# Token setup of an early-fusion kernel: GpSimd rounds the angles and makes V, the third magnitude is made with the other two, and its sine group goes first

## The reference

```python
dt = jnp.exp(log_dt)                          # 256 channels
w = -jnp.exp(log_w_real) + 1j * w_imag        # 256 x 64
dtA = w * dt[:, None]
Cm = Cc * (jnp.exp(dtA) - 1.0) / w            # Cc: 8 x 256 x 64, complex input
K = jnp.einsum('chn,hnl->chl', Cm, jnp.exp(dtA[:, :, None] * jnp.arange(512)))
h = 2 * K.real                                # 8 x 256 x 512
...
h = concatenate([h, txt], axis=1)             # 8 x 384 x 512
h = h + attention(layernorm(h)); h = h + experts(layernorm(h))
```

## Time and profile before

| | |
|---|---|
| Median of 3 runs | 885.98 us (883.85 to 888.88) |
| Profiled execution | 892.42 us, of which the span in the trace is 890.6 |
| Busy in the span | PE 775.7, DVE 509.7, ACT 366.0, POOL 344.2 us |
| PE's first matmul of the chunks | 73.75 us after the start of the span |

### The profile page before, as it was taken

How to read it: one execution, slowest core, us unless ns; L and a number is a source line. 1 busy time by engine, 2 the same in 40 slices (tenths; PEclk the granted TensorE clock), 3 DMA queues, 4 the chain that set the end, 5 groups by cost and what they waited for, 6 DMA issues and landing times.

```text
span 890.6 us, 19870 instructions
## 1 busy us (share of the span) xinstructions
PE 775.7 (87%) x7181; PEld 489.7 (55%) x7182; DVE 509.7 (57%) x927; ACT 366.0 (41%) x637; POOL 344.2 (39%) x356
## 2 busy tenths in 40 slices
PE   0007999879989999999999789999999999999993
PEld 0007998655455455564554446666666666666661
DVE  7997755786884756667744425453444444444441
ACT  4772423425225261443323324554444444444440
POOL 0036765051280030300267614444444545454441
PEclk9999999999999999999999999999999999999997
DMA  5011216134164051967524254454544444554442
GB/s 204 0 47 49 71 44 228 48 88 117 59 145 93 30 156 40 211 168 181 117 70 129 75 170 77 81 91 79 93 73 92 73 92 75 90 77 88 81 72 35
DMA packets 67645, 84.76 MB, mean 95 GB/s; under 512 B 37664, under 2 KB 37792, under 8 KB 66944
## 3 DMA queue, kind: packets, MB, share of 16 engines
q0 software_dynamic: 14080, 29.53, 19.0%
q1 hardware_dynamic: 41408, 31.42, 13.0%
q10 hardware_dynamic: 12096, 22.94, 9.6%
HBM read 48.43 MB, written 27.63 MB: 85 GB/s over the span
## 4 chain that ended last, share of the span: by engine, by line
PE 75%; DVE 12%; ACT 5%; issue 2%; POOL 2%; another core or an unknown queue 2%; DMA 2%; DVEq 0%; ACTq 0%; POOLq 0%
PE PS L2137 11%; PE PS L2139 11%; PE PS L2138 11%; PE PS L1101 8%; PE PS L1103 8%; PE PS L1102 7%; PE PS L607 7%; PE PS L2147 3%; PE PS L762 2%; PE PS L2169 2%; DVE big L1020 1%; DVE big L1457 1%; DVE work L1462 1%; PE PS L1314 1%
## 5 line engine op out<-in xcount | busy, mean ns | idle before, releaser
L2137 PE MATMUL PS<-big,work 128*128 x605 | 200.4, 331 | 3.7 <-ACT work L2215 2.4
L2139 PE MATMUL PS<-big,work 128*128 x605 | 200.8, 332 | 0.0
L2138 PE MATMUL PS<-big,work 128*128 x605 | 200.6, 332 | 0.0
L2256 DVE SCALAR_TENSOR_TENSOR work<-work,PS 128x352 f32<-128x352 f32 x55 | 28.7, 521 | 150.8 <-PE PS L2139 150.8
L2324 POOL DMA_INDIRECT out_dram<-work x55 | 88.2, 1604 | 59.4 <-DVE work L2294 49.0
L2215 ACT ACTIVATE work<-PS 128x1024 f16<-128x1024 f16 x55 | 56.3, 1023 | 86.0 <-PE PS L2147 86.0
L1706 POOL DMA_INDIRECT slots_dram<-work x48 | 50.1, 1043 | 84.8 <-DVE work L2053 62.5
L2137 PEld LDWEIGHTS PS<-big,work 128*128 128x128 f16 x605 | 59.2, 98 | 42.3 <-issue 7.2
L2139 PEld LDWEIGHTS PS<-big,work 128*128 128x128 f16 x605 | 59.2, 98 | 41.9 <-issue 0.6
L2138 PEld LDWEIGHTS PS<-big,work 128*128 128x128 f16 x605 | 59.1, 98 | 36.0 <-issue 0.6
L2311 POOL DMA_INDIRECT big<-x_dram,work x55 | 54.7, 995 | 46.6 <-POOL work L2308 44.8
(11 more groups left out here) (276 smaller groups left out, 1652.0 us busy)
## 6 DMA issues: line engine op xcount, KB each, us to landing
work<-in_weights ACTq DMA_DIRECT2D x31, 272.0 KB
work<-in_shared ACTq DMA_DIRECT2D x28, 256.0 KB, 3.3
big<-in_weights ACTq DMA_DIRECT2D x25, 272.0 KB, 3.3
x_dram<-big SPq DMA_DIRECT2D x24, 256.0 KB, 2.4
out_dram<-big SPq DMA_DIRECT2D x24, 256.0 KB, 4.6
big<-in_weights SPq DMA_DIRECT2D x1, 2176.0 KB, 10.3
big<-in_par SPq DMA_DIRECT2D x1, 1185.0 KB, 10.3
big<-in_c_real SPq DMA_DIRECT2D x1, 1024.0 KB, 5.5
```

The source lines that it names most:

```text
L2137: pe.matmul(out, x_high, w_high, start=start, stop=False)
L2138: pe.matmul(out, x_high, w_low, start=False, stop=False)
L2139: return pe.matmul(out, x_low, w_high, start=False, stop=stop)
L2256: v.scalar_tensor_tensor(a, a, 1 / (X_SCALE * W_SCALE * W_SCALE), PS[:, UB[u], 0:F], ALU.mult, ALU.mult).then_inc(m.mul, 1)
```

## The change

`kt`, the rounding, goes from DVE to POOL for all three groups; DVE keeps `gt`. `V`, three instructions of 2,048 columns (now `A2`, `B2`, `V`), goes from DVE to POOL as well; DVE keeps the three of `U`. The partial products go to tiles of their own (`V_SUB`, `U_ADD`, which are the two buffers of `P1`). `MAG_B` is made straight after `MAG_ZW`, ahead of the table of sines. The groups are taken in the order 2, 0, 1. The waits follow: POOL's `cos2` waits for ACT's cosine of group 2; DVE's multiplications wait for each group's cosine; DVE's first `P1` waits for POOL's `cos2`, its first `P2` for `sin2`, its second `P1` for `V`.

```diff
@@ -222,6 +222,7 @@
         assert R2 + 10 * Q <= NB * BLK
         SA = [cut(work, k * H, H) for k in range(16)]
         P1 = [cut(work, 16 * H + u * Q, Q) for u in range(2)]
+        V_SUB, U_ADD = P1
         assert Q == HC * PW
 
 
@@ -249,17 +250,16 @@
         def htile(i, w):
             return htok[:, slot_of(i, w), :]
 
-        GROUPS = range(3)
+        GROUPS = (2, 0, 1)
         set_v = steps("set_v", [
             "xk", "xk2", "xf", "xf2", "xnum", "xden", "xrec", "xe", "xbits", "x", "rho", "rho8", "rho64", "s", "k", "k2", "s1", "s2", "s3", "r", "r2"]
             + [f"{x}{k}" for k in "zw" for x in ("n", "m", "f")]
             + ["a2", "b2", "m2", "im2", "den", "rden", "em", "sh2", "emsh", "t2", "er", "t3", "ei", "p1", "p2", "p3", "Dr", "p4", "p5", "p6", "Di",
                "al0", "al1", "be0", "be1"]
-            + [f"{x}{g}" for g in GROUPS for x in ("kt", "gt")]
-            + ["A1", "A2", "B1", "U", "B2", "V"] + [f"{x}{g}" for g in range(2) for x in ("sin", "cos")])
-        set_a = steps("set_a", ["xt", "th", "mag_zw", "sh", "ch"] + [f"t{g}" for g in GROUPS]
-                      + [f"{x}{g}" for g in GROUPS for x in ("sin", "abs", "cos")] + ["mag_b"])
-        set_g = steps("set_g", ["wsum", "cos2", "sin2"])
+            + [f"gt{g}" for g in GROUPS] + ["A1", "B1", "U"] + [f"{x}{g}" for g in range(2) for x in ("sin", "cos")])
+        set_a = steps("set_a", ["xt", "th", "mag_zw", "mag_b", "sh", "ch"] + [f"t{g}" for g in GROUPS]
+                      + [f"{x}{g}" for g in GROUPS for x in ("sin", "abs", "cos")])
+        set_g = steps("set_g", ["wsum"] + [f"kt{g}" for g in GROUPS] + ["A2", "B2", "V", "cos2", "sin2"])
         wb_a = steps("wb_a", ["kv_sum", "kv_mean", "kv", "c_sum", "c_mean", "c", "wb"])
         wb_p = steps("wb_p", ["wb"])
         CHUNKS = range(NCHUNK)
@@ -290,7 +290,8 @@
             sp.dma_start(par, a["par"]).then_inc(s_par, 16)
             sp.dma_start(rope, a["rope"]).then_inc(s_rope, 16)
             sp.dma_start(gate_T[:], a["gate_T"]).then_inc(s_gate, 16)
-            sp.wait_ge(set_v.sem, set_v.at("V"))
+            sp.wait_ge(set_g.sem, set_g.at("V"))
+            sp.wait_ge(set_v.sem, set_v.at("U"))
             sp.dma_start(htok[:, 22:24, :], a["txt"][:, 0:2, :]).then_inc(s_txt[0], 16)
             sp.dma_start(TXT_T0.rearrange("p a t -> p (a t)"), a["txt_T"][:, 0:AW * P]).then_inc(s_txt_T[0], 16)
 
@@ -300,6 +301,9 @@
             sp.wait_ge(cm_p.sem, cm_p.at("c0"))
             sp.dma_start(TXT_T1[:, 1:3].rearrange("p k a t -> p (k a t)"), a["txt_T"][:, 2 * AW * P:]).then_inc(s_txt_T[2], 16)
             sp.dma_start(htok[:, 12:22:3, :], a["txt"][:, 4:8, :]).then_inc(s_txt[2], 16)
+
+        def over_b(x):
+            return x.unsqueeze(2).broadcast_to([P, H, B])
 
         def by_8(x):
             return x.rearrange("p (h a) -> p h a", a=AW)
@@ -313,13 +317,16 @@
             for j in range(AW):
                 last = act.activation(by_8(MAG_ZW)[:, :, j], RHOB[:, 0:2 * H], ACT.Exp, scale=float(j))
             last.then_inc(set_a.now("mag_zw"), 1)
+            for j in range(AW):
+                last = act.activation(by_8(MAG_B)[:, :, j], RHO, ACT.Exp, scale=float(j))
+            last.then_inc(set_a.now("mag_b"), 1)
 
             act.wait_ge(set_v.sem, set_v.at("r2"))
             act.wait_ge(s_early, 16)
             act.activation(SH, R, ACT.Sin, scale=SIN_PI).then_inc(set_a.now("sh"), 1)
             act.activation(CH, R, ACT.Sin, scale=SIN_PI, bias=ec("half_pi_low")).then_inc(set_a.now("ch"), 1)
-            act.wait_ge(set_v.sem, set_v.at("fw"))
             for g in GROUPS:
+                act.wait_ge(set_v.sem, set_v.at(("fz", "fw", "r2")[g]))
                 for j in range(AW):
                     out = by_8(TURN[:, g * Q:(g + 1) * Q])[:, :, j]
                     if g == 2:
@@ -334,10 +341,6 @@
                 act.activation(TURN[:, part], KT[:, part], ACT.Abs).then_inc(set_a.now(f"abs{g}"), 1)
                 act.wait_ge(set_a.sem, set_a.at(f"abs{g}"))
                 act.activation(COS[:, part], TURN[:, part], ACT.Sin, scale=-2 * SIN_PI, bias=ec("half_pi")).then_inc(set_a.now(f"cos{g}"), 1)
-            for j in range(AW):
-                last = act.activation(by_8(MAG_B)[:, :, j], RHO, ACT.Exp, scale=float(j))
-            last.then_inc(set_a.now("mag_b"), 1)
-
             act.wait_ge(s_par, 16)
             act.wait_ge(set_g.sem, set_g.at("wsum"))
             for x, part, mean in (("kv", pc("to_kv"), ec("centre_kv")), ("c", pc("compress_T"), ec("centre_c"))):
@@ -416,8 +419,18 @@
         def tok_gpsimd(pool):
             pool.wait_ge(s_par, 16)
             pool.tensor_tensor(pc("out_res_T"), pc("to_kv"), pc("out_res_T"), ALU.add).then_inc(set_g.now("wsum"), 1)
-            pool.wait_ge(set_v.sem, set_v.at("V"))
+            for g in GROUPS:
+                part = slice(g * Q, (g + 1) * Q)
+                pool.wait_ge(set_a.sem, set_a.at(f"t{g}"))
+                pool.tensor_scalar(KT[:, part], TURN[:, part], MAGIC, MAGIC, ALU.add, ALU.subtract).then_inc(set_g.now(f"kt{g}"), 1)
+            pool.wait_ge(set_v.sem, set_v.at("be1"))
+            pool.wait_ge(s_c, 32)
+            pool.tensor_tensor(hc(V), hc(CR), over_b(BE), ALU.mult).then_inc(set_g.now("A2"), 1)
             pool.wait_ge(set_a.sem, set_a.at("mag_b"))
+            pool.tensor_tensor(hc(V_SUB), hc(CI), over_b(AL), ALU.mult).then_inc(set_g.now("B2"), 1)
+            pool.wait_ge(set_g.sem, set_g.at("B2"))
+            pool.tensor_tensor(V, V, V_SUB, ALU.subtract).then_inc(set_g.now("V"), 1)
+            pool.wait_ge(set_a.sem, set_a.at("cos2"))
             pool.tensor_tensor(B1, B1, MAG_B, ALU.mult).then_inc(set_g.now("cos2"), 1)
             pool.tensor_tensor(B2, B2, MAG_B, ALU.mult).then_inc(set_g.now("sin2"), 1)
             pool.wait_ge(set_v.sem, set_v.at("cos1"))
@@ -543,39 +556,36 @@
             v.tensor_scalar(BE[HALF:P], X1[HALF:P], -1.0, None, ALU.mult).then_inc(set_v.now("be1"), 1)
             for g in GROUPS:
                 part = slice(g * Q, (g + 1) * Q)
-                act_done(f"t{g}")
-                v.tensor_scalar(KT[:, part], TURN[:, part], MAGIC, MAGIC, ALU.add, ALU.subtract).then_inc(set_v.now(f"kt{g}"), 1)
-                own()
+                dve.wait_ge(set_g.sem, set_g.at(f"kt{g}"))
                 v.tensor_tensor(KT[:, part], KT[:, part], TURN[:, part], ALU.subtract).then_inc(set_v.now(f"gt{g}"), 1)
 
             dve.wait_ge(s_c, 32)
-            over = lambda x: x.unsqueeze(2).broadcast_to([P, H, B])
-            v.tensor_tensor(hc(U), hc(CR), over(AL), ALU.mult).then_inc(set_v.now("A1"), 1)
-            v.tensor_tensor(hc(V), hc(CR), over(BE), ALU.mult).then_inc(set_v.now("A2"), 1)
-            own()
-            v.tensor_tensor(hc(CR), hc(CI), over(BE), ALU.mult).then_inc(set_v.now("B1"), 1)
-            own()
-            v.tensor_tensor(U, U, CR, ALU.add).then_inc(set_v.now("U"), 1)
-            v.tensor_tensor(hc(CI), hc(CI), over(AL), ALU.mult).then_inc(set_v.now("B2"), 1)
-            own()
-            v.tensor_tensor(V, V, CI, ALU.subtract).then_inc(set_v.now("V"), 1)
+            own()
+            v.tensor_tensor(hc(U), hc(CR), over_b(AL), ALU.mult).then_inc(set_v.now("A1"), 1)
+            v.tensor_tensor(hc(U_ADD), hc(CI), over_b(BE), ALU.mult).then_inc(set_v.now("B1"), 1)
+            own()
+            v.tensor_tensor(U, U, U_ADD, ALU.add).then_inc(set_v.now("U"), 1)
             act_done("mag_zw")
-            act_done("cos1")
             for g in range(2):
                 part = slice(g * Q, (g + 1) * Q)
+                act_done(f"cos{g}")
                 v.tensor_tensor(SIN[:, part], SIN[:, part], MAG_ZW[:, part], ALU.mult).then_inc(set_v.now(f"sin{g}"), 1)
                 v.tensor_tensor(COS[:, part], COS[:, part], MAG_ZW[:, part], ALU.mult).then_inc(set_v.now(f"cos{g}"), 1)
             own()
-            dve.wait_ge(set_g.sem, set_g.at("sin2"))
+            dve.wait_ge(set_g.sem, set_g.at("cos2"))
 
             for n in CHUNKS:
                 u = n % 2
+                if n == 1:
+                    dve.wait_ge(set_g.sem, set_g.at("V"))
                 if n >= 2:
                     dve.wait_ge(tok_p.sem, tok_p.at(f"mm{n - 2}b"))
                 dve.wait_ge(tok_t.sem, tok_t.at(f"zw_{n}"))
                 v.tensor_tensor(grid(P1[u]), table(4 + u, HC * 8).unsqueeze(3).broadcast_to([P, HC, 8, 8]), fast(B1, n), ALU.mult).then_inc(
                     tok_v.now(f"P1_{n}"), 1)
                 if u == 0:
+                    if n == 0:
+                        dve.wait_ge(set_g.sem, set_g.at("sin2"))
                     dve.wait_ge(tok_t.sem, tok_t.at(f"wi_{n}"))
                     v.tensor_tensor(grid(P2[u]), table(6, 0).unsqueeze(3).broadcast_to([P, HC, 8, 8]), fast(B2, n), ALU.mult).then_inc(
                         tok_v.now(f"P2_{n}"), 1)
```

## The result

The changed kernel takes 911.12 us (median of 4 runs, 910.83 to 913.96), the kernel before 885.24 us in the same comparison (4 runs): a ratio of 1.030, 95% interval 1.027 to 1.033. It is slower by 25.9 us, nearly twice the 13.4 that were forecast, and outside of the range.

The account below looks back on a forecast made before the run. PE bounds the kernel, its start set by two nearly equal setup chains, on DVE and over ACT and POOL. The terms moved that start from 73.75 to 87.2 us; 13.4 us added to the 885.98 median gave 899.4, range 892 to 907.

Parts of the forecast that it names:

- The mechanism: Setup: DVE and POOL alternate whole instructions on SBUF operands, also at 2,048 columns; PSUM operands go free; chance 0.80.
- A period: Setup from be1 on: one instruction each of POOL and DVE in turn, 5.75 us with broadcast operands, 6.2 without.
- term (1) of the sum: DVE's small chain: three POOL roundings hold it, so be1 ends at 38.8 us instead of 32.55.
- The rival with a slow rounding: Setup roundings: POOL's rounding exceeds 4.5 us, each further us costs 3 or more, 907 us and up; chance 0.03.
- the upper bound: Whole sum with rounding 4.5 us and POOL's two-input instructions 4.53 us everywhere: 21 us later, 907 us.
- k: Price of one 2,048-column rounding on POOL in the setup, not in the trace, taken as 2.3 us.
- (2): Setup from be1 to U: six DVE and five POOL instructions alternate, 2.05 plus 30.1 us, U ending at 71.0.
- (3): DVE's four multiplications after U, with a PSUM operand, go unheld at 2.2 us each, ending at 79.8.
- (4): From the last multiplication to PE's start: table copy and three products, 7.4 us, PE starting at 87.2.
- The shift is passed on: After PE's start: PE's progress releases everything, so the 13.4 us later start reaches the end at full size.
- Magnitude hidden: Setup on ACT: eight Exp, 3.73 us, moved ahead of the sines delay SH and CH, hidden with 1.6 us to spare.

Follow-up runs that it names:

- E3: Changed kernel with roundings and V both back on DVE; early third magnitude, group order 2, 0, 1 and waits kept: ratio 1.010 to the kernel before.
- E4: As E3, but POOL's two multiplications by the third magnitude wait for V as before the change: ratio 1.0015 to the kernel before.
- E1: Changed kernel with the three roundings back on DVE, V staying on POOL: ratio 1.015 to the kernel before.
- E8: As E1, but POOL starts only after DVE's U and makes cos2, sin2, then V: ratio 1.004 to the kernel before.
- E10: Changed kernel with each POOL rounding as a conversion to a 32-bit integer: one run, 906.28 us beside 895.59 for the kernel before.
- E6: Changed kernel with the last four small DVE instructions written with two SBUF inputs: one run, 907.70 us beside 884.01 for the kernel before.
- E2: Changed kernel with V back on DVE, the roundings staying on POOL: ratio 1.028 to the kernel before.
- E9: As E4, but U and V made in halves, the second behind chunk 1's products and shared between DVE and POOL: ratio 0.9989 to the kernel before.

## Why the prediction was wrong

- **The mechanism was right.** DVE and POOL take turns on SBUF operands, whole instructions of 2,048 columns are held as 512 were, PSUM operands go free. E3 against E4 and E1 against E8 show it without any change in work. A period, one instruction of each engine, of 5.75 us for broadcast operands measured 5.84 and 5.69, that of 6.2 us 6.45, 6.54 and 5.85.
- **The step that failed is the price of the rounding on POOL**, term (1) of the sum. It said: from below the casts, from above "the slowest two-input instruction of this width, 4.53 us", and "I take 2.3, near the cast, which also has one input". POOL's tensor_scalar takes 7.15 us, outside of both bounds. Three of them held the small chain until 50.5, where 38.8 was forecast: 11.7 of the 12.2 us by which the start was missed. The bound from above was none: a one-input instruction needn't be cheaper than a two-input one. The rival with a slow rounding named this very case and its direction, 907 us and 3 more for each us beyond 4.5 (so 915 with 7.15, where 911.12 was measured), and had a chance of 0.03; E10 shows that the forecast was nearly that of a kernel with casts, in part by luck. The sum of the upper bound is also wrong: k 4.5 and 4.53 everywhere give 3 x 2.2 + 2 x 0.83 + 3 x 0.36 = 9.3 more than 13.4, so 22.7 us and 908.7, not 21 and 907; the measured time is outside of that too. The Trainium skill, GPSIMD Engine Reference, section 4.1 (Engine selection), calls GpSimd roughly line-rate with one input; the cast agrees with it at 1.9 us, the tensor_scalar at 5.4 and 7.15 doesn't, and the measurement decides.
- **Each hold was not k.** The sum took three times k less 0.65; with 7.15 that gives 53.3. L537, with two SBUF inputs, ended 4.9 us after the start of a rounding of 7.25, and the chain ended at 50.5. E6 shows that this hangs on the kind of instruction. The Trainium skill, SBUF — State Buffer, section "Who interferes with whom", has the loser blocked for the whole instruction; beside POOL's two-input instructions the traces agree (2.15 us from its end to the end of DVE's), beside its tensor_scalar a copy or a tensor_scalar of DVE is held to the end as well (7.05 us), but a two-input instruction ends earlier, and there the measurement decides.
- **(2) From be1 to U**: 32.2 us forecast, 32.6 measured (50.5 to 83.1), six DVE and five POOL instructions in turn. **(3)** four multiplications: 8.8, measured 8.8. **(4)** 7.4, measured 7.5.
- **The shift is passed on**: 25.7 us at the start, 25.9 in the medians. That they agree so closely is partly chance. In E1, E2 and E3 the start is 11.8, 21.3 and 7.2 us later and the ratio is worth 13.4, 25.5 and 8.5, and in the profiles the stages behind vary by up to 10.
- **By parts**, from the starts: early magnitude, order and waits 80.9 - 73.7 = 7.2 (E3); V on POOL 85.5 - 80.9 = 4.6 (E1); the roundings 95.0 - 80.9 = 14.1 (E2); together 25.9, where 25.7 were measured, so they add up.
- **Magnitude hidden**: right. SH and CH came 3.9 us later and delayed nothing.

## What to carry to other kernels

Work moved from VectorE to GpSimd takes VectorE's time all the same while both have their operands in SBUF: count each GpSimd instruction at its full duration on VectorE's chain, and place it beside instructions with a PSUM operand, or gate it with a wait, if it is to be free. Removing a wait can be the loss (E3 against E4). A price for an operation that the trace doesn't show is not bounded by another operation that looks heavier; where the sum takes it three times, the range has to hold a multiple of it, or it is measured first.

## What the runs showed of the hardware that was not expected

- GpSimd's tensor_scalar on 128 x 2,048 f32: 5.38 us with one operation, 7.15 with two; its conversion to integer 1.9; its two-input instruction 3.7 with a broadcast operand, 3.8 to 4.5 without.
- Beside a tensor_scalar of GpSimd, VectorE's small two-input instructions end 4.8 to 4.9 us after the start of its 7.15 us, or 3.9 after the start of its 5.38; a copy or a tensor_scalar ends only with it.
- The stage behind the chunks took between 59 and 69 us, with the granted clock at 0.50 for 0 to some 25 us of it, whether the chunks ended earlier, at the same time or later than before. E9's gain of 5.6 us ahead of that stage could not be seen in the program's time (ratio 0.9989).
